# Splat attention block with channel mixing, one core: the last chunk but one gets its output product, transposes and mixing inside the main loop

## What is computed

```python
q_weights = exp(sum((q - centers)**2) * inv_var)          # k alike
logits = einsum('bihs,bjhs,hs->bijh', q_weights, k_weights, amplitudes)
out = einsum('bijh,bjhd->bihd', softmax(logits / temp, axis=2), v)
x = x + out @ out_w.T
h = layernorm(x);  h_prev = h shifted by one row
xr = mu_r * h + (1 - mu_r) * h_prev                       # xk alike, with mu_k
x = x + sigmoid(xr @ W_r) * (square(relu(xk @ W_k)) @ W_v)
```

## Time and profile before

| what | value |
|---|---|
| median of three runs | 2189.22 us |
| the profiled execution's own time | 2189.85 us |
| its span, first to last instruction | 2188.1 us |
| TensorE matmul busy | 2145.8 us (98%) |
| ScalarE busy | 2005.2 us (92%) |
| VectorE busy | 887.0 us (41%) |
| GpSimd busy | 389.7 us (18%) |

### The profile page before, as it was taken

One profiled execution on the slowest core, in us unless ns is written; L12 is line 12 of the kernel. 1 busy time (PEld: TensorE's weight loads), 2 busy tenths in 40 slices (PEclk: granted clock), 3 DMA queues, 4 the chain that ended last, 5 costly groups with the idle time before them and its releaser, 6 DMA issues.

```text
span 2188.1 us, 47111 instructions
## 1 busy us (share of the span) xinstructions
PE 2145.8 (98%) x20220; PEld 900.5 (41%) x20220; DVE 887.0 (41%) x1868; ACT 2005.2 (92%) x2194; POOL 389.7 (18%) x490
## 2 busy tenths in 40 slices
PE   8999999999999999999999999999999999999998
PEld 5434444444444444444443333333334343444445
DVE  5244454444443454354433235233242423334335
ACT  3899999999989999999999999999999999999995
POOL 0234433443120201233401101010200000000001
PEclk9999999999999999999999999999999999999999
DMA  6645535462340523336423042301151130301111
GB/s 177 159 126 150 148 122 126 133 161 87 96 116 19 155 69 69 112 92 162 123 48 92 26 110 64 85 26 42 45 134 47 31 86 20 81 18 49 43 40 40
DMA packets 176453, 193.00 MB, mean 88 GB/s; under 512 B 88640, under 2 KB 108480, under 8 KB 176224
## 3 DMA queue, kind: packets, MB, share of 16 engines
q1 hardware_dynamic: 166960, 174.96, 28.9%
q0 software_dynamic: 7168, 14.69, 2.9%
q10 hardware_dynamic: 2096, 0.14, 0.1%
HBM read 99.03 MB, written 75.94 MB: 80 GB/s over the span
## 4 chain that ended last, share of the span: by engine, by line
PE 85%; ACT 13%; DVE 1%; issue 0%; DMA 0%; POOL 0%; DVEq 0%; POOLq 0%
PE ps_pv L826 37%; PE ps_scores L807 25%; PE ps_step L854 16%; ACT probs L1143 13%; PE ps_step L871 2%; PE ps_scores L839 1%; PE ps_scores L844 1%; PE ps_step L833 0%; PE ps_scores L848 0%; PE ps_scores L849 0%; DMA x_prep<-x 0%; DVE den_all L1667 0%; ACT weight L1207 0%; DVE weight L1425 0%; ACT weight L1170 0%
## 5 line engine op out<-in xcount | busy, mean ns | idle before, releaser
L1143 ACT ACTIVATE probs<-ps_scores 128x1024 f32<-128x1024 f32 x2048 | 1928.9, 1034 | 118.3 <-PE ps_scores L807 111.7
L826 PE MATMUL ps_pv<-probs,vals 128*32 128x512 f32 (+1 forms) x8600 | 1060.9, 583 | 2.5 <-DVE o_raw L1515 0.9
L807 PE MATMUL ps_scores<-q_aug,k_aug 49*128 49x512 f32 x4096 | 720.5, 441 | 20.5 <-ACT probs L1143 16.1
L807 PEld LDWEIGHTS ps_scores<-q_aug,k_aug 49*128 49x128 f32 x4096 | 333.0, 184 | 689.0 <-ACT probs L1143 643.8
L826 PEld LDWEIGHTS ps_pv<-probs,vals 128*32 128x32 f32 x8600 | 298.9, 140 | 282.8 <-issue 177.1
L1273 POOL DMA_DIRECT2D packed<-qk x224 | 113.9, 514 | 820.4 <-DVE qk L1448 787.1
L1278 POOL TENSOR_TENSOR packed<-qk 32x512 f32<-32x512 f32 x224 | 235.7, 1052 | 16.9
L1654 DVE RECIPROCAL den_all<-den_all 128x128 f32<-128x128 f32 x252 | 223.8, 924 | 0.6
L1283 POOL TENSOR_TENSOR k_act<-k_act 128x512 f32<-128x512 f32 x28 | 29.8, 1063 | 892.6 <-DVE k_act L1451 892.6
L1515 DVE COPY o_raw<-ps_pv 128x512 f32<-128x512 f32 x64 | 44.3, 692 | 322.2 <-PE ps_pv L826 322.2
L854 PE MATMUL ps_step<-h_t,wqkv 128*32 128x256 f32 x1600 | 106.1, 382 | 0.0
(11 more groups left out here) (212 smaller groups left out, 1013.9 us busy)
## 6 DMA issues: line engine op xcount, KB each, us to landing
k_aug<-k_parts SPq DMA_DIRECT2D x128, 192.0 KB, 4.2
q_aug<-q_parts SPq DMA_DIRECT2D x128, 192.0 KB
k_parts<-parts SPq DMA_DIRECT2D x32, 512.0 KB, 3.4
q_parts<-parts SPq DMA_DIRECT2D x32, 512.0 KB, 3.9
packed<-qk POOLq DMA_DIRECT2D x224, 64.0 KB, 2.3
x_ffn<-x SPq DMA_DIRECT2D x18, 512.0 KB, 4.3
k_parts<-parts SPq DMA_DIRECT2D x32, 256.0 KB, 4.0
q_parts<-parts SPq DMA_DIRECT2D x32, 256.0 KB, 4.2
```

Source lines behind the costliest of these rows:

```text
L807: mm = pe.matmul(ps_scores[:, g % RING, e, :], k_aug[rows, s % 2, pair, kt * P:(kt + 1) * P], q_aug[rows, u % 2, pair, :], start=True, sto ...
L826: mm = pe.matmul(ps_pv[32 * c:32 * c + 32, at], vals[:, s % 2, kt, :, c], probs[:, tick % PROB_SLOTS, c, at], start=(kt == 0), stop=(kt == ...
L1143: act.activation(probs[:, tick % PROB_SLOTS, 2 * pair:2 * pair + 2, :], ps_scores[:, g % RING, :, :], ACT.Exp).then_inc(probs_ready, 1)
```

## The change

The `ffn` queue becomes a list of blocks (`blocks_of`). Chunk 3,1 keeps its first nine steps together, then come `LAST_BUT`'s `out0` and `out1`, then chunk 3,1's `v1`, then `LAST_BUT`'s `turn0` and `turn1`. At block ends within batch 3 the next block may begin one tick after the last, where it was four. `LAST_BUT`'s mixing goes to VectorE's list in the loop, all four parts on the tick behind `turn1`. Behind the loop, both transposes of `LAST_BUT`, ScalarE's eviction and scaling of them, GpSimd's additions and one small copy on VectorE (`carry`) are gone. `r0` is issued first of all there, ahead of `LAST`'s output product, and `r1` behind it. `full` is false for the pair of gaps in which a unit ends.

```diff
+def blocks_of(tasks):
+    if LAST_BUT not in tasks:
+        return [(task, steps_of(task)) for task in tasks]
+    *early, before, last = [(task, steps_of(task)) for task in tasks]
+    return early + [(before[0], FFN_STEPS[:9]), (LAST_BUT, FFN_STEPS[:2]), (before[0], FFN_STEPS[9:]), (LAST_BUT, FFN_STEPS[2:4])]
...
-                if kind == "ffn" and step == 0 and part == 0:
+                if name == "out0" and part == 0:
                     done = max(UNIT_OF[task[1], s, task[2]] for s in range(STAGES))
                     ready = max(ready, KT * (done + 1) + OUT_TICKS[task[1] == NB - 1])
...
                         at, step = at + 1, 0
                         ready = tick + 4
+                        if task[:2] == LAST_BUT[:2] and at < len(tasks):
+                            ready = tick + 1
+                            if tasks[at][1][0] == "turn0":
+                                ready = max(ready, span[LAST_BUT, "out1"][1] + 1 + FFN_GAP["turn0"])
...
 def full(gap):
     work = PIECES_AT.get(name_of(gap), ())
-    return sum(not name.startswith("turn") for _, name, _ in work) >= (3 if gap % 2 else 1)
+    return sum(not name.startswith("turn") for _, name, _ in work) >= (3 if gap % 2 else 1) and not 3 * (gap // 2) % KT == 1
...
-MIX_AT = beside((later(end(task, "turn1") + (1, 1, 2, 3)[part]), (task, part)) for task in FFNS if task != LAST_BUT for part in range(4))
+MIX_AT = beside((later(end(task, "turn1") + (1, 1, 2, 3)[part]) if task != LAST_BUT else end(task, "turn1") + 1, (task, part))
+                for task in FFNS for part in range(4))
...
@@ TensorE, behind the loop @@
-            pe.wait_ge(ffn_ln, LN_STEPS * n)
-            closing("turn0", 4)
-            closing("turn1", 5)
+            pe.wait_ge(step_free, SIDE_STEPS)
+            pe.wait_ge(mix_steps, MIX * (n - 1) + 5)
+            closing("r0", 7)
...
-            pe.wait_ge(step_free, SIDE_STEPS)
             pe.wait_ge(pv_free, UNITS)
-            pe.wait_ge(last_added, 2)
-            closing("r0", 7)
             closing("r1", 6)
             pe.wait_ge(last_evicted, 1)
-            pe.wait_ge(last_added, 4)
+            pe.wait_ge(mix_steps, MIX * n)
             closing("k0", 0)
             closing("k1", 1)
...
@@ ScalarE, behind the loop @@
-            act.wait_ge(last_mixed, 1)
-            last_turned(1)
...
-            last_old(0)
-            last_new(0, mixed_r)
-            last_old(1)
-            last_new(1, mixed_k)
-            for pair, bank in ((0, 7), (1, 6)):
-                act.wait_ge(last_mm, 5 + pair)
+            for pair, bank, step in ((0, 7, 1), (1, 6, 4)):
+                act.wait_ge(last_mm, step)
                 last_gate(pair, bank)
...
@@ GpSimd, behind the loop @@
-            for which, to in ((0, mixed_r), (1, mixed_k)):
-                for half in range(HALVES):
-                    pool.wait_ge(last_copied, 5 + 4 * which + half)
-                    pool.tensor_tensor(to[:, half, :], to[:, half, :], last_tmp[2 * which + half], ALU.add).then_inc(last_added, 1)
-                    pool.wait_ge(last_added, 2 * which + half + 1)
...
@@ VectorE, behind the loop @@
-            v.wait_ge(mix_steps, MIX * (n - 1))
-            carry(LAST_BUT).then_inc(last_mixed, 1)
```

More of the change, by code:

```diff
@@ L142, in lay_side_work @@
     maxima = sorted(max_gap(u) for u in FIRST_UNIT.values() if u)
-    state = {"prep": [preps, 0, 0, 0, 0], "ffn": [ffns, 0, 0, 0, 0]}
+    state = {"prep": [blocks_of(preps), 0, 0, 0, 0], "ffn": [blocks_of(ffns), 0, 0, 0, 0]}
     def due(state):
@@ L148, in due @@
             return EVENT_TICKS
-        kind, b, i = tasks[at]
+        kind, b, i = tasks[at][0]
         if kind == "late":
@@ L169, in lay_side_work @@
                     continue
-                task = tasks[at]
-                steps = steps_of(task)
+                task, steps = tasks[at]
                 name = steps[step]
                 turn = name.startswith("turn")
-                if kind == "ffn" and step == 0 and part == 0:
+                if name == "out0" and part == 0:
                     done = max(UNIT_OF[task[1], s, task[2]] for s in range(STAGES))
@@ L1115, in _ @@
             closing("v1", 3)
-            pe.wait_ge(last_copied, 12)
-            pe.wait_ge(last_mixed, 4)
+            pe.wait_ge(last_copied, 2)
+            pe.wait_ge(last_mixed, 3)
             closing("k0", 7)
             closing("k1", 6)
-            pe.wait_ge(last_copied, 16)
-            pe.wait_ge(last_mixed, 6)
+            pe.wait_ge(last_copied, 6)
+            pe.wait_ge(last_mixed, 5)
             closing("r0", 4)
@@ L1226, in last_gate @@
                                scale=0.5).then_inc(last_copied, 1)
-            before = FFNS[FFN_NO[LAST_BUT] - 1]
-            act.wait_ge(last_mixed, 1)
-            last_turned(1)
-            act.wait_ge(last_copied, 2)
-            act.wait_ge(mix_steps, MIX * FFN_NO[LAST_BUT])
-            act.wait_ge(step_mm, max(STEP_NO[before, name] for name in ("k1", "v1")) + 1)
-            last_old(0)
-            last_new(0, mixed_r)
-            last_old(1)
-            last_new(1, mixed_k)
-            for pair, bank in ((0, 7), (1, 6)):
-                act.wait_ge(last_mm, 5 + pair)
+            for pair, bank, step in ((0, 7, 1), (1, 6, 4)):
+                act.wait_ge(last_mm, step)
                 last_gate(pair, bank)
             for half in range(HALVES):
-                act.wait_ge(last_mm, 7 + half)
+                act.wait_ge(last_mm, 5 + half)
                 act.activation(k_act[:, half, :], banks[half], ACT.Relu).then_inc(last_copied, 1)
[L1247 to L1250, removed]
+            act.wait_ge(last_mixed, 1)
+            last_turned(7)
+            act.wait_ge(last_copied, 6)
             last_old(1)
@@ L1254, in _ @@
             for pair, bank in ((0, 4), (1, 5)):
-                act.wait_ge(last_mm, 15 + pair)
+                act.wait_ge(last_mm, 13 + pair)
                 last_gate(pair, bank)
@@ L1284, in _ @@
                         pool.wait_ge(k_squared, 2 * FFN_NO[task] + half + 1)
-            for which, to in ((0, mixed_r), (1, mixed_k)):
-                for half in range(HALVES):
-                    pool.wait_ge(last_copied, 5 + 4 * which + half)
-                    pool.tensor_tensor(to[:, half, :], to[:, half, :], last_tmp[2 * which + half], ALU.add).then_inc(last_added, 1)
-                    pool.wait_ge(last_added, 2 * which + half + 1)
             for half in range(HALVES):
-                pool.wait_ge(last_copied, 13 + half)
+                pool.wait_ge(last_copied, 3 + half)
                 pool.tensor_tensor(k_act[:, half, :], k_act[:, half, :], k_act[:, half, :], ALU.mult).then_inc(last_squared, 1)
@@ L1673, in _ @@
             for pair in range(2):
-                v.wait_ge(last_mm, 3 + pair)
+                v.wait_ge(last_mm, 2 + pair)
                 rows = x_ffn[:, n % 2, 2 * pair:2 * pair + 2, :]
@@ L1679, in _ @@
                 layernorm("ffn", n, x_ffn[:, n % 2, :, :], h_ffn, ffn_ln, part)
-            v.wait_ge(last_copied, 10)
+            v.wait_ge(mix_steps, MIX * n)
             carry(LAST).then_inc(last_mixed, 1)
-            v.wait_ge(last_mm, 8)
+            v.wait_ge(last_mm, 6)
             for nth, part in enumerate((2, 3, 0, 1)):
-                v.wait_ge(last_copied, 17 + nth)
+                v.wait_ge(last_copied, 7 + nth)
                 mixed(part, last_tmp[part]).then_inc(last_mixed, 1)
-            v.wait_ge(last_copied, 12)
+            v.wait_ge(last_copied, 2)
             v.wait_ge(out_stored, 16 * (n - 1))
             for pair, bank in ((0, 2), (1, 3)):
-                v.wait_ge(last_mm, 11 + pair)
+                v.wait_ge(last_mm, 9 + pair)
                 gated(pair, banks[bank]).then_inc(last_evicted, 1)
@@ L1693, in _ @@
             for half, bank in ((0, 7), (1, 6)):
-                v.wait_ge(last_mm, 13 + half)
+                v.wait_ge(last_mm, 11 + half)
                 relu_squared(half, banks[bank], half + 1).then_inc(last_evicted, 1)
@@ L1697, in _ @@
             for pair, bank in ((0, 0), (1, 1)):
-                v.wait_ge(last_copied, 21 + pair)
-                v.wait_ge(last_mm, 17 + pair)
+                v.wait_ge(last_copied, 11 + pair)
+                v.wait_ge(last_mm, 15 + pair)
                 gated(pair, banks[bank]).then_inc(last_evicted, 1)
```

7 lines of the change are left out of this document (removed).

## The result

The changed kernel takes 2192.23 us (median of 21 runs, 2190.63 to 2194.08) and the kernel before 2189.32 us (21 runs, 2188.27 to 2190.21). The ratio is 1.0014, with a 95% interval of 1.0008 to 1.0020: slower by 2.9 us. The forecast was 2190.0 with a range of 2187.7 to 2192.2. The median lies just above it, and the loss of 0.14% is clear of the noise where I had forecast +0.75 us. It is within 0.2%, to which I had given 0.94.

What follows compares the result with a forecast made beforehand. It took TensorE to bound pairs with product steps, ScalarE the empty ones, and a chain of small waits the part behind the loop. Terms +0.5 + 1.35 + 0.6 - 1.7 = +0.75 gave 2190.0 us, range 2187.7 to 2192.2.

Steps and rivals of the forecast that it cites:

- The plan: Schedule in the loop: chunk 3,1 starts three ticks earlier, `LAST_BUT`'s `turn0` at tick 1016, `turn1` 1017, two empty pairs left.
- The pairs in the loop: From tick 974 on, a pair of transposes replaces one empty pair: +0.5 us, kept 0.5 to 1.1.
- VectorE's new wait: At `turn1` in the loop, TensorE waits 1.0 to 1.5 us for VectorE's copy of `turn0`: +1.35 us, kept 0 to 1.8.
- The side weights: Seven of ScalarE's 56 weights move by one pair, three into light pairs: +0.6 us, kept -0.2 to +0.9.
- Behind the loop: GpSimd's additions go, so the last unit's product, layer norm and `LAST`'s transposes start earlier: -1.7 us, kept -1.2 to -2.2.
- The rule that I weighed against this step: VectorE and GpSimd lock shared ports, so the last scaling ends some 0.45 us later; whole sum 1.2 instead of 0.75.
- The clock: TensorE idles some 2 us ahead of `LAST`'s transposes and drops to 1.2 GHz for 6.9 us, costing 3.4: 2193.4 us; chance 0.06.
- The sum: All terms for the whole kernel: +0.5 + 1.35 + 0.6 - 1.7 = +0.75 us, 2190.0 us on the median.
- The backlog spreads: In the loop `turn0` waits as well and moved weights meet late evictions, +1.5 more: 2191.5 to 2192.5 us; chance 0.13.

Runs made afterwards that it cites:

- the later addition: The changed kernel with VectorE's last addition of chunk 3,1 one tick later, behind the eviction of `turn0`: 2190.22 us, ratio 1.0007 to the kernel before.
- the three edits together: The changed kernel with ScalarE doing the squares, chunk 3,1's last addition behind `turn0`'s eviction, and the old `full`: 2187.49 us, ratio 0.9990 to the kernel before.
- The filled kernel: The changed kernel with 22 unit-matrix transposes added in TensorE's wait behind `k1` of `LAST_BUT`: 2191.64 us, and 2191.67 us when run again.
- the longer wait: The changed kernel with eight fills of unused tiles on VectorE ahead of the last chunk's scalings: 2196.95 us, ratio 1.0037 to the kernel before.

## Why the prediction was wrong

- **The plan**: right. All steps stand at the ticks that I had worked out, and `turn0` of `LAST_BUT` starts without a wait.
- **The pairs in the loop** (+0.5): right. Without the wait and at equal weights, the changed loop is 0.6 us longer from tick 974 on, by the profiles with the later addition and with the three edits together.
- **VectorE's new wait** (+1.35, kept 0 to 1.8): right in place, releaser and cause, a little too large. I had 12.9 us from the eviction of `out1` to the end of `turn0`'s copy; it is 2142.58 + 0.69 - 2130.75 = 12.5. It costs 0.9 to 1.0 us.
- **The side weights** (+0.6, kept to +0.9): right in sign and cause, mis-sized. They cost 1.1 to 1.4, above my bound. I took 0.25 us for each of three in light pairs and left out the 0.2 at the unit's end behind. The 0.15 that I took off for the four that shift among full pairs doesn't show either.
- **Behind the loop** (-1.7, kept -1.2 to -2.2): this step failed. With a full clock it is 36.5 against 37.4, -0.9. The start was right: the second scaling is at 0.42, and the layer norm starts 1.05 us earlier in relation to the loop's end, where I had 0.9. What failed is the meeting of the norm with GpSimd's squares, for which I added 0.5 us (1.39 to 1.9). The squares did come 2.8 us earlier, as I had said. In the kernel before, the first one stands here:

```profile
2167.04 1.04 POOL L1294 TENSOR_TENSOR k_act<-k_act 128x512 f32<-128x512 f32 x1 [4.66 <-ACT k_act L1245]
```

Three us earlier it ends at 2165.1, ahead of the scalings at 2165.2 and right over the Newton steps. I put that meeting at nothing. It cost 0.73 us, and the second square's meeting with the scalings 0.72 (2.10 instead of 1.38), together 1.45 instead of 0.5. So the transposes of `LAST` start 0.45 us earlier, not 1.2. The wait for the squares is gone as forecast, and the value products start 1.1 us earlier. At the very end 0.3 of that is lost again, a term that I didn't have and whose cause stays open.
- **The rule that I weighed against this step.** The Trainium skill ("SBUF — State Buffer", "Who interferes with whom") has the loser wait out the other's whole instruction. The Newton step ends at 2166.90, as GpSimd's square does at 2166.88, so the trace agrees. I had worked the rule out for the scalings alone, as two of four parts left behind the second square, with a sum of 1.2. In the trace 0.79 us of scalings are left behind it, a little over two parts. That estimate was nearer than mine and lacked the Newton step as well.
- **The clock** (a rival at 0.06): it fell in four of six profiles of the changed kernel, but for 3.4 us and 1.6 us of cost, half the price I gave. I had seen the wait of "some 2 us" and set its chance by the kernel before, which had waited 1.69 us at full clock; it became 2.73 us, by the Newton step above. The Trainium skill ("TensorE: Matmul & The Clock Gate", "What's actually happening") says that idleness lowers the clock. The trace agrees in five of the nine profiles with this wait, and in the other four the clock stayed up.
- **The sum.** Measured terms are +0.6, +1.0, +1.1 to 1.4 and -0.9. The profiles as a whole give +1.9 at a full clock (2.7 in the loop, -0.9 behind it), and +3.5 where the clock falls. Of the 1.15 us between +0.75 and +1.9, the step behind the loop makes 0.8, the side weights 0.5 to 0.8 and the pairs 0.1, less the 0.4 by which the wait was too large. The range had no room for both and the clock in one direction.
- **A number that fits by luck.** *The backlog spreads* had 2191.5 to 2192.5, and the median is 2192.2. But `turn0` didn't wait, so it isn't what happened.

What stays open: the share of the fall in the median of +2.9. The filled kernel has a full clock in both profiles and is still 2.2 and 2.4 us above the kernel before. Runs with a mean clock of 0.999, like with like, say the same: 2190.6 in both of the changed kernel against 2188.3 on average in the 28 of the kernel before, +2.3. So the fall adds 0.3 to 0.6 to the median, and most of the loss is there without it. Between the +1.9 of the profiles and these +2.2 to +2.4, 0.1 lies outside the span (the time is 1.87 us above it, where it was 1.80); the rest isn't explained. That the fall has to do with the wait is supported by the longer wait (twice as long in its profile, and a lower mean clock in four of five runs). The two filled profiles without a fall are too few to show it, as four of nine unfilled ones have none either.

## What to carry to other kernels

When work leaves a tail that several engines share, ask what the freed engine waits for next and what then runs beside it, the small operations of that wait included. Here GpSimd's squares, worth 0.5 us while TensorE was busy, fell onto the late chain and cost 1.75 of the 2.6 us that could be gained behind the loop. A step that is moved into a full loop brings its evictions with it, and one long instruction of an in-order engine ahead of such an eviction is a wait of its own; its place in the list is free to choose. Work of an engine should stand where that engine is idle anyway, and that can be the unit's end.

## What the runs showed of the hardware

- A wait of TensorE of 2.73 us was followed by 3.4 us at the lower clock in five of nine profiles, one of 6.02 us by 6.8 us, and waits of 1.28 us by none in two. The same binary did it in some executions and not in others.
- A VectorE multiply of 128x4 that takes 0.16 us took 0.89 beside GpSimd's multiply of 128x512, and ended with it to 0.02 us.
- The changed loop of 2075 us repeats to 0.3 us in ten profiles. What scatters more is the start, by 2 us, and with it the median of the whole.
- From the end of VectorE's last addition to the end of the span it is 2.88 to 2.89 us in all twelve profiles of changed kernels in which GpSimd squares behind the loop, and 2.57 to 2.58 in the other six. Why isn't shown.
